# Tile 0's query and key projection placed inside the patch steps, late input normalised on VectorE, GpSimd's first part in another order

## The reference

```python
xn = _layernorm(x)
x = x + _L0_attn_ref(xn, Wqkv, Wout, bout) + _L0_ffn_ref(xn, wqkv, ...)
```

```python
h = shift_token(x)               # half of the features from the token before
q, k, v = jnp.split(h @ wqkv, 3, axis=-1)      # 8 heads of 64
q, k = l2norm(q) * qs, l2norm(k) * ksc
q, k = rotary_xpos(q, k)         # cosine and sine tables with a scale
o = local_attention(q, k, v)     # windows of 64, each sees itself and the one before
x = x + o @ wo
```

## Time and profile before

| what | value |
|---|---|
| median of 3 runs | 386.66 us (386.44 to 388.58) |
| the profiled execution | 386.01 us, of which the span is 384.2 |
| granted TensorE clock, mean | 0.98 |
| PE busy | 348.4 us (91%) |
| PEld busy | 267.3 us (70%) |
| ACT busy | 288.8 us (75%) |
| DVE busy | 275.3 us (72%) |
| POOL busy | 254.2 us (66%) |

### The profile page before, as it was taken

The page is one execution under the profiler, slowest core; times in us unless marked ns, Lnnn a source line. Parts: engine busy times, 40 slices in busy tenths (PEclk is TensorE's granted clock), DMA queues, the critical chain, the costliest instruction groups (busy, mean ns, idle before and its releaser), DMA issues. The chain is left out here.

```text
span 384.2 us, 10815 instructions
## 1 busy us (share of the span) xinstructions
PE 348.4 (91%) x4015; PEld 267.3 (70%) x4015; DVE 275.3 (72%) x480; ACT 288.8 (75%) x889; POOL 254.2 (66%) x244
## 2 busy tenths in 40 slices
PE   1868689999999999999979679999999999999996
PEld 0656557888888888666456458787888887766565
DVE  4557777888788778468588768887888788465543
ACT  2567379989989998976726578888989989876421
POOL 2998588999999999620234578888898989420000
PEclk9999899999999999999989969999999999999999
DMA  6976123222322322540000112223222322200011
GB/s 189 365 163 186 67 70 71 56 64 63 71 52 63 74 60 50 154 150 15 2 0 0 43 41 50 56 57 78 56 62 63 70 54 65 64 7 15 9 45 55
DMA packets 35314, 27.63 MB, mean 72 GB/s; under 512 B 19093, under 2 KB 29247, under 8 KB 34751
## 3 DMA queue, kind: packets, MB, share of 16 engines
q1 hardware_dynamic: 34975, 26.49, 25.8%
q10 hardware_dynamic: 288, 0.46, 0.4%
HBM read 9.64 MB, written 1.05 MB: 28 GB/s over the span
## 5 line engine op out<-in xcount | busy, mean ns | idle before, releaser
L1185 ACT ACTIVATE probs<-ps,neg_max 128x128 f32<-128x128 f32 x256 | 90.1, 377 | 7.3 <-DVE neg_max L1411 6.7
L635 POOL TENSOR_TENSOR qkn<-work 128x512 f32<-128x512 f32 x64 | 80.9, 1286 | 9.9 <-DVE work L1367 5.4
L649 POOL TENSOR_TENSOR probs_n<-probs,row_inv 128x512 f32<-128x512 f32 x64 | 66.8, 1043 | 24.1 <-DVE row_inv L1416 22.4
L643 POOL TENSOR_TENSOR qkn<-qkn,rnorm 128x512 f32<-128x512 f32 x64 | 65.5, 1044 | 19.8 <-ACT rnorm L1141 19.3
L1185 ACT ACTIVATION_READ_ACCUMULATOR probs<-ps,neg_max 128x1 f32 x256 | 55.2, 216 | 0.0
L1134 ACT ACTIVATE work<-ps 128x1024 f32<-128x1024 f32 x32 | 32.8, 1026 | 15.3 <-issue 12.7
L172 PE MATMUL ps<-wqkv_hi,h_hi 128*128 128x512 f32 x96 | 42.9, 447 | 1.6 <-ACT work L1134 1.6
L1357 DVE TENSOR_REDUCE ss_pair<-work 128x16 f32<-128x1024 f32 x32 | 39.0, 1219 | 7.3 <-ACT work L1134 5.6
L1411 DVE TENSOR_REDUCE neg_max<-ps 128x4 f32<-128x512 f32 x64 | 41.0, 682 | 3.2 <-PE ps L844 3.1
L858 PE MATMUL ps<-small,probs_n 128*128 128x128 f32 x256 | 37.7, 286 | 3.8 <-ACT q_t L1167 3.3
L1367 DVE TENSOR_TENSOR work<-ps,cos_w 128x1024 f32<-128x1024 f32 x32 | 38.8, 1211 | 3.1 <-PE ps L174 3.1
(11 more groups left out here) (154 smaller groups left out, 743.8 us busy)
## 6 DMA issues: line engine op xcount, KB each, us to landing
v_off<-v_tok SPq DMA_DIRECT2D x64, 128.0 KB, 2.3
k_t<-k_t SPq DMA_DIRECT2D x30, 128.0 KB, 2.4
cos_w<-in_cos_t SPq DMA_DIRECT2D x2, 1024.0 KB, 7.8
sin_w<-in_sin_t SPq DMA_DIRECT2D x2, 1024.0 KB, 10.7
x_shift<-x SPq DMA_DIRECT2D x64, 32.0 KB, 1.9
x_raw<-in_x SPq DMA_DIRECT2D x4, 256.0 KB, 4.6
x<-xin SPq DMA_DIRECT2D x8, 128.0 KB, 5.0
x_shift<-in_wqkv SPq DMA_DIRECT2D x1, 768.0 KB, 8.9
```

The source lines that it names most:

```text
L635: pool.tensor_tensor(to, first, second[:, :, ::-1, :], ALU.add).then_inc(rot_summed, 1)
L643: pool.tensor_tensor(of, of, rnorm[:, part * HEADS:(part + 1) * HEADS].unsqueeze(2) .broadcast_to([P, HEADS, DH]), ALU.mult).then_inc(rot_ ...
L649: pool.tensor_tensor(probs_n[:, 4 * g:4 * g + 4, :], probs[:, 4 * g:4 * g + 4, :], row_inv[:, 4 * g:4 * g + 4].unsqueeze(2).broadcast_to([ ...
L1185: e = act.activation(probs[:, k, :], s_ps[g][:, cw * P:(cw + 1) * P], ACT.Exp, bias=neg_max[:, k:k + 1], accum_out=row_sum[:, k:k + 1])
```

## The change

On ScalarE, both halves of the weight rounding and `round_first(0)` stand in step 0; the second query and key chunk is taken in step 1 instead of 0; `round_first(1)` stays near its place, 2 and 3 are in step 4, the masks in step 3. Tile 0's queries are projected at the end of TensorE's step 4 and its keys at the end of step 5, both into bank 6, 512 columns each (`project_first`); the second waits until the first is rotated and squared. VectorE rotates the halves in steps 5 and 6 (`rotate_first`), into `x1_shift` instead of `rot1` and `rot2`, ScalarE squares them in the same steps, into `x_patch` (`square_first`), and the sums of squares stand at the end of VectorE's step 6. `inverse_norms(0)` follows ScalarE's copy in step 7. At the hand-over TensorE projects tile 1 where it projected tile 0. The query and key chunks have 280 tokens first and then 264 and 240, which share bank 6. VectorE normalises groups 2 and 3. GpSimd does the cosine table, the weight remainder and `split_first(0)` before it repeats patches 1 and 2. TensorE no longer waits for the second chunk before `weigh_patch_values(0)`.

```diff
@@ -50,6 +50,8 @@
 A_STEPS = -(-PATCHED // A_STEP)
 A_CHUNK = 272
 A_COLS = 2 * A_CHUNK
+A_Q_CHUNKS = [(0, 280), (280, A_COLS - 280)]
+A_K_CHUNKS = [(0, 280), (280, PATCHED - 280)]
 A_VAL = 36
 TURN_FIRST = 4
 W_PARTS = 2
@@ -313,7 +315,8 @@
         ffn_ps = bank(5)
         tr_ps = bank(2)
         a_s = bank(0, 4).rearrange("p (g c) -> p g c", g=4)[:, :, 0:4 * PATCH]
-        a_qk_ps = [(bank(0), bank(1)), (bank(6), bank(7))]
+        a_qk_ps = [(bank(0), bank(1)), (bank(6), bank(6)[:, A_Q_CHUNKS[1][1]:])]
+        first_ps = bank(6)
         a_vr = bank(4)
         a_tp = bank(5)
...
@@ -433,6 +438,16 @@
             first = g * WIDE + (q // 2) * (WIDE // 2)
             return rows, slice(at + first, at + first + WIDE // 2), slice(1 + first, 1 + first + WIDE // 2)
 
+        def rot_of(n):
+
+            if isinstance(n, int) and n == 0:
+                return x1_shift[:, 1:1 + 2 * INNER], x1_shift[:, 1 + 2 * INNER:1 + 4 * INNER]
+            return rot1, rot2
+
+        def sq_of(n):
+
+            return x_patch[:, 0:2 * INNER] if isinstance(n, int) and n == 0 else sq
+
         block = ctx.enter_context(nc.Block())
 
...
-            def normalize_input(g):
-
-                pool.wait_ge(rstd0_done, g + 1)
-                for t in range(4 * g, 4 * g + 4):
-                    pool.tensor_scalar(xn_tok[:, t, :], x_raw[:, t, :], mv[:, t, 0:1], rstd0[:, t:t + 1],
-                                       ALU.subtract, ALU.mult).then_inc(xn_late, 1)
-
-            pool.wait_ge(xin0_done, 1)
-            repeat_patches(0)
-            normalize_input(2)
-            normalize_input(3)
-            pool.wait_ge(xin0_done, 2)
-            repeat_patches(1)
-            repeat_patches(2)
-
             def scale_table(table, table_in):
 
                 pool.wait_ge(table_in, 16)
...
+            pool.wait_ge(xin0_done, 1)
+            repeat_patches(0)
             pool.wait_ge(scale_in, 32)
             scale_table(cos_w, cos_in)
             split_wqkv()
+            split_first(0)
+            pool.wait_ge(xin0_done, 2)
+            repeat_patches(1)
+            repeat_patches(2)
             scale_table(sin_w, sin_in)
-            for g in range(SPANS):
+            for g in range(1, SPANS):
                 split_first(g)
             pool.wait_ge(h_split, SPANS)
...
 
+            def project_first(part):
+
+
+                if part == 0:
+                    pe.wait_ge(h_split, 1)
+                    pe.wait_ge(wqkv_split, 1)
+                    pe.wait_ge(xin0_done, SPANS)
+                else:
+                    pe.wait_ge(first_q_squared, 1)
+                span = slice(part * INNER, (part + 1) * INNER)
+                matmul3(pe, first_ps, input_tile(0), (wqkv_hi[:, 0, span], wqkv_lo[:, 0, span])).then_inc(
+                    qk_ready if part else first_q_ready, 1)
+
             def project_patch_qk(chunk):
-                span = slice(1 + chunk * A_CHUNK, 1 + (chunk + 1) * A_CHUNK)
                 pe.wait_ge(xin0_done, chunk + 1)
                 q_ps, k_ps = a_qk_ps[chunk]
-                pe.matmul(q_ps[:, 0:A_CHUNK], a_wqkv_s[:, 0:DIM], xin[:, span], start=True, stop=True)
-                pe.matmul(k_ps[:, 0:A_CHUNK], a_wqkv_s[:, DIM:2 * DIM], xin[:, span],
+                (q_at, q_size), (k_at, k_size) = A_Q_CHUNKS[chunk], A_K_CHUNKS[chunk]
+                pe.matmul(q_ps[:, 0:q_size], a_wqkv_s[:, 0:DIM], xin[:, 1 + q_at:1 + q_at + q_size],
+                          start=True, stop=True)
+                pe.matmul(k_ps[:, 0:k_size], a_wqkv_s[:, DIM:2 * DIM], xin[:, 1 + k_at:1 + k_at + k_size],
                           start=True, stop=True).then_inc(a_qk_done, 1)
 
             def project_patch_values(t):
...
@@ -751,8 +770,6 @@
                 after(pe, a_pt_done, t + 1)
                 after(pe, a_v_done, t + 1)
                 after(pe, a_o_done, t)
-                if t == 0:
-                    pe.wait_ge(a_qk_taken, 2)
                 for g in range(QUADS):
                     for j in patch_rows(t):
                         mm = pe.matmul(a_op[32 * j:32 * j + 32, g, :],
@@ -786,6 +803,8 @@
                     project_patch_qk(1)
                 if there(t - 1, A_STEPS):
                     weigh_patch_values(t - 1)
+                if t in (4, 5):
+                    project_first(t - 4)
 
             def in_front(t):
                 if t == -1:
@@ -795,14 +814,11 @@
                     project_patch_qk(0)
                     turn_input(1)
                 if t == A_STEPS:
-
-                    pe.wait_ge(wqkv_split, 1)
                     pe.wait_ge(a_dif_done, A_STEPS)
-                    project_qk(0, 0)
+                    project_qk(0, 1)
 
             over_patches(pe, patch_step, in_front)
             turn_patch_out(0)
-            project_qk(0, 1)
             turn_patch_out(1)
             pe.wait_ge(a_o_done, A_STEPS)
             pe.wait_ge(masks_done, 1)
...
@@ -1110,22 +1126,34 @@
                     act.activation(a_p, a_dif[:], ACT.Exp).then_inc(a_p_done, 1)
 
                 if t == 0:
+                    act.wait_ge(wqkv_in[0], 16)
+                    for part in range(W_PARTS):
+                        round_part(0, part * W_PART)
+                    round_first(0)
+                if t == 1:
                     take_patch_qk(1)
                 if t in (2, 3):
                     take_input(t)
-                if t in (0, 1):
-                    if t == 0:
-                        act.wait_ge(wqkv_in[0], 16)
-                    round_part(0, t * W_PART)
-                if t in (2, 3, 4, 5):
-                    round_first(t - 2)
-                if t == 4:
+                if t == 2:
+                    round_first(1)
+                if t == 3:
                     act.wait_ge(masks_in, 16)
                     act.copy(masks[:], masks_f).then_inc(masks_done, 1)
-                if t == 6:
+                if t == 4:
+                    round_first(2)
+                    round_first(3)
+                if t in (5, 6):
+                    square_first(t - 5)
+                if t == A_STEPS:
+                    inverse_norms(0)
                     act.wait_ge(w1_in, 16)
                     for other in range(LAYERS):
                         act.copy(w1_hi[:, other, :], w1_raw[:, other, :]).then_inc(w1_rounded, 1)
+
+            def square_first(part):
+                act.wait_ge(rot_done if part else first_q_rotated, 2)
+                act.activation(sq_of(0)[:, part * INNER:(part + 1) * INNER], first_ps, ACT.Square).then_inc(
+                    sq_done if part else first_q_squared, 1)
 
             def norms(n):
                 after(act, qk_ready, n + 1)
@@ -1152,8 +1180,6 @@
                     input_rstd(3)
 
             over_patches(act, patch_step, in_front)
-            norms(0)
-            inverse_norms(0)
 
             for layer in range(LAYERS):
                 def take_v(n, parity):
@@ -1349,15 +1375,35 @@
                     patch_differences(t)
                 if there(t - 2, A_STEPS):
                     patch_out(t - 2)
+                if t in (5, 6):
+                    if t == 5:
+                        dve.wait_ge(wqkv_split, 1)
+                        dve.wait_ge(tables_done, 4)
+                    rotate_first(t - 5)
                 if there(t, A_STEPS):
                     patch_values(t)
+                if t == 0:
+                    normalize_input(3)
+                if t == 6:
+                    sum_squares(0)
 
             def sum_squares(n):
                 after(dve, sq_done, n + 1)
-                dve.reduce_sum(ss, sq[:].rearrange("p (h d) -> p h d", d=DH), AX.X).then_inc(ss_done, 1)
+                dve.reduce_sum(ss, sq_of(n).rearrange("p (h d) -> p h d", d=DH), AX.X).then_inc(ss_done, 1)
                 after(dve, ss_done, 2 * n + 1)
                 after(dve, lnss_done, n)
                 dve.tensor_reduce(ssc[:], ss_pair[:], AX.X, ALU.max).then_inc(ss_done, 1)
+
+            def rotate_first(part):
+
+
+
+                dve.wait_ge(qk_ready if part else first_q_ready, 1)
+                for table, to in zip((cos_w, sin_w), rot_of(0)):
+                    dve.tensor_tensor(to[:, part * INNER:(part + 1) * INNER].rearrange("p (h d) -> p h d", d=DH),
+                                      first_ps.rearrange("p (h d) -> p h d", d=DH),
+                                      table[:, 0, part, :].unsqueeze(1).broadcast_to([P, HEADS, DH]),
+                                      ALU.mult).then_inc(rot_done if part else first_q_rotated, 1)
 
             def rotate(n, t, table):
+                    normalize_input(2)
                     dve.wait_ge(const_in, 16)
                     dve.wait_ge(a_ones_done, 2)
                     dve.wait_ge(zeroed, 9)
 
             over_patches(dve, patch_step, in_front)
-            dve.wait_ge(tables_done, 4)
-            rotate(0, 0, cos_w)
-            rotate(0, 0, sin_w)
             patch_out(A_STEPS - 1)
```

(24 more changed lines are left out.)

## The result

Median of 14 runs 391.65 us against 386.63 us of the kernel before (14 runs on the same chip). The ratio is 1.0108 (95% interval 1.0079 to 1.0137): the changed kernel is 1.1% slower, 4 to 5 us. The forecast was 392.8 us, slower with a chance of 0.83.

What follows compares the result with a forecast made beforehand. The patch steps' ring of engine hand-overs, up to tile 0's inverse norms, was taken to set the time. Terms 4.0 + 0.9 + 0.2 + 1.0 = 6.1 on 386.0 gave 392.1, plus 0.65 for the median: 392.8 us, range 388.5 to 395.5.

Steps and rivals of the forecast that it cites:

- Step 1: ScalarE, ready for the first input rounding at 17.4, waits 5.6 us for the shifted input, landing at 23.0.
- Step 2: ScalarE's wait delays the patch loop: scores of step 3 at 28.1 instead of 24.13; 2.3 to 4.0 us, 4.0 taken.
- rival B: Wait paid, but TensorE's 1.67 us gap in step 3's scores hidden and clock cost little: 389 to 391 us; chance 0.22.
- signs: Trace marks expected, including step 3's scores at 28 to 30 and the second query and key half at 24.5.
- Edits taken as nothing: Small moves counted as free, including VectorE's normalisations in idle time before steps 0 and 1's scores; 2 us at most.
- Step 3: TensorE's clock drops after its 4.6 us idle stretch, up to the scores of step 3; at most 1.8 us, 0.9 taken.
- Steps 4 and 5: Tile 0's early projection inside the patch steps costs 0.2 us; lower clock on six matmuls at the patches' end, 1.0.
- rival D: Tile 0's early projection pays if the last turn is not held up at the hand-over; 385.0 us, chance 0.07.
- rival C: Shifted input lands in time for ScalarE's rounding, at 17.4; 386.2 to 387.4 us, chance 0.09.
- The sums: Terms total 6.1 us on the profiled 386.0; range from 388.5 to 395.5, plus the time intervals given for rivals.

Runs made afterwards that it cites:

- e6: e5 with ScalarE's rounding of group 0 put back in step 0, as in the changed kernel; ratio to the kernel before 1.0091.
- e5: Changed kernel, but GpSimd starts its tables after VectorE's four normalisations and splits group 0 later, and ScalarE rounds group 0 in step 1; ratio 1.0039 to the kernel before.
- e1: Changed kernel with group 0's rounding moved behind the second query and key chunk in step 1, its GpSimd split behind the sine table; ratio 1.0097 to the kernel before.
- e7: e5 with TensorE turning the last probabilities before it projects tile 1; ratio to the kernel before 1.0080.
- e10: e5 with tile 0's value projection moved in front of tile 1's projection on TensorE; ratio to the kernel before 1.0049.
- e12: e9 with tile 0's value projection moved early as in e10; ratio to the kernel before 1.0112.
- e4: Changed kernel with tile 0 projected, rotated and squared behind the patch steps as before; ratio to the kernel before 1.0174.
- e11: Kernel before with only tile 0's value projection moved in front of tile 1's projection on TensorE; ratio to the kernel before 0.9998.
- e9: Kernel before with only tile 0's projection, rotation, square and sums moved inside the patch steps, plus what that needs; ratio to the kernel before 1.0079.
- e8: e5 with tile 0's hand-over behind the patch steps as before; ratio to the kernel before 1.0078.
- e3: Changed kernel with e1's later rounding of group 0 and group 3's normalisations in front of the first patch step; ratio to the kernel before 1.0060.

## Why the prediction was right or wrong

- **Step 1** held: 5.13 us idle, ended by the DMA at 22.71; 5.6 and 23.0 had been said.
- **Step 2** has nearly the right sum from the wrong parts. Steps 2 and 3 gave 4.9 at the scores of step 3, all to the wait; the maxima of step 3 are 5.68 late. The wait with its clock is 2.34 of that (e6 against e5), the contention on top of it 3.71 (the changed kernel against e6), and e5 with neither is 0.37 ahead of the kernel before. At the exponent of step 1 the wait costs 3.35; behind it TensorE's gap is hidden, as rival B had said, and 2.3 was the lower bound given for this. Two of the signs failed: the scores of step 3 came at 31.63, not 28 to 30, and the second query and key half at 26.41, not 24.5.
- **The failed step is "Edits taken as nothing"**: "eight short instructions, some 2 us together, in VectorE's idle time". Four of them took 8.18 us. The bound put beside them, 2 us of cost, was too low: the contention costs 3.71 us at the maxima of step 3 and 3.35 at the logarithm even with the wait beside it. It counted VectorE's own time and not what GpSimd does meanwhile, and the cover it relied on ("step 1 then waits for ScalarE anyway") ends 2.2 us too early: ScalarE was ready at 23.8, VectorE's differences at 26.0. The earlier trace rows hold no VectorE copy or tensor_scalar next to a long GpSimd instruction; the sign was in the rest of the trace of the kernel before, where four such normalisations take 1.12 us when GpSimd is idle (from 6.38) and 1.51 when it is not (from 9.82). The Trainium skill (SBUF — State Buffer, SBUF: two separate sides) has the rule: VectorE in a 2-port mode and GpSimd share a pair of ports under an exclusive lock, held for a whole instruction. The three pairs of rows above agree with it instruction by instruction. That GpSimd's work is the cause e5 shows, by moving it away; that it is a lock on ports, and that these instructions run in such a mode, no run shows.
- **The two causes cover each other.** Without the wait alone the logarithm moves by 0.02 (e1); without the contention alone (e6, where one remainder on GpSimd moved too) by 3.35, and tile 0's scores by 1.9; without both by 5.23, and the scores by 3.5 (e5). By the ratios only the last is clear of the changed kernel's: 1.0097 and 1.0091 against 1.0108, and 1.0039. So the agreement of 391.65 with 392.8 is no proof of step 2. It is luck: the wait was charged too high, and the contention, which was charged nothing, made up for it.
- **Step 3** held, and was larger: the lower level from 25.3 to 32.1, with the values at 1.91 and the turn at 1.11. From the scores of step 2 to those of step 3 it is 5.49 us, against 2.68 before (21.45 to 24.13, without the gap); half of 1.8 had been counted. In e6, which has the wait and not the contention, the clock is low too (0.50 from 23.3 to 26.5, the values at 1.46).
- **Steps 4 and 5** gave 1.2; the trace has 1.15 (5.68 at the maxima of step 3, 6.83 at the logarithm). The size is near, the place isn't: the low stretch came not at the six matmuls, which start 0.23 apart where 0.43 had been said, but at the three before them, the turn and the values of step 6. That the last copy stands between the sums and the logarithm was seen as written (49.82, then 50.30), but removing it brings nothing (e7), so rival D's place was wrong too: in e7 what ends this stage is TensorE's queue in front of tile 0's turn. GpSimd's scaling lies close behind it, since taking the values out of that queue (e10 to e12) gives only about 0.1 us.
- **What came back later** (1.0 of 6.7) had not been foreseen.
- **The sums** have small slips that decide nothing: rival C's upper end is 387.2 (386.65 - 0.7 + 1.2), not 387.4; the range's upper end adds up to 395.35; and the 0.4 taken off at its lower end comes from no row.

What stays open: what the "issue" gaps in TensorE's stream depend on. The DMA views of these profiles give a lead that no run tests. They have a queue named "instruction", and each gap at the two places ends 2.2 to 3.0 us after a packet of 0.02 MB began on it: 23.5 and 26.14, 33.8 and 36.01 in the kernel before, 23.2 and 25.77 in e5, 23.5 and 26.09 in e7, 40.3 and 42.73 in e4. Where TensorE reaches the place later than that, there is no gap (packet at 23.9, step 3's scores at 31.63 in the changed kernel). It would explain why a long wait before the place hides the gap.

## What to carry to other kernels

Before an instruction is moved to an engine's idle time, look at what the engines beside it run at that moment, not only at its own queue: for VectorE's SBUF-to-SBUF operations with scalars that means GpSimd's long instructions. A cast or copy that waits for a DMA should stand where the landing time in the trace already lies behind it, or everything in the engine's order pays for it. And where two causes lie side by side, remove both before judging either: by the time each alone seemed worth nothing or little here (1.0097 and 1.0091 against 1.0108), both together were worth 0.7%. And read a small edit at the mark next to it: in e1 it was 1.1 us ahead there, and 2.70 instead of 1.46 us for six matmuls at the lower clock hid that at the next mark.

## What was not expected of the hardware

- A VectorE tensor_scalar of 128x128 in SBUF, 0.28 us by itself, took 2.38, 3.46 and 1.30 us beside GpSimd tensor_tensor instructions of 2.35, 3.42 and 1.26 us, ending 0.07 to 0.09 us after each; the GpSimd instructions kept their length.
- Idle times of TensorE named "issue": 1.67 and 0.67 (before), 1.28 and 0.67 (e11), 1.56 (e5), 2.01 (e7), 1.77 (e9), 1.00 (e10), 1.61 (e12), 2.25 (e4), 0.38 and 2.32 (e8), each at one of two places in the program (inside step 3's scores, inside step 6's values), and one of 0.26 in e6, in front of step 6's turn. There is none in the changed kernel, e1 and e3, where TensorE had waited 3.96 to 4.81 us for ScalarE or VectorE before step 3.
